# A new order of the work in one step of a fused recurrent block, with two squares and one product moved to VectorE

## The chip, the cores and the metric

The kernel runs on one core of a Trainium2 chip. The metric is the device time in microseconds (us) of one execution, as the median of a few runs. The profiled execution is one run of its own; its span and its engine rows come from the hardware profiler.

## What is computed

`x` holds 32 sequences of 256 tokens with 128 channels (8192 rows), all in float32. `xn` is the layer norm of `x`. Two branches start from it. The first is a time mix with the recurrent WKV sum over the tokens, followed by a channel mix; the second is a mixture of experts with one shared expert and, per token, one of eight routed experts (the top one, with input scaled by the sigmoid of its logit).

```
h  = ln(x);  xk, xv, xr = mixes of h and h one token before
k, v, r = xk @ Wk, xv @ Wv, sigmoid(xr @ Wr)
rwkv = r * wkv(k, v)                 # running max, exponentials, two scans, one division
x  = x + rwkv @ Wo
h  = ln(x);  xk, xr = mixes of h and h one token before
kk = square(relu(xk @ Fk))           # 128 -> 512 channels
x  = x + sigmoid(xr @ Fr) * (kk @ Fv)
out = x_in + x * silu(shared_expert(xn) + routed_expert(xn))
```

## The kernel before

The 8192 tokens are cut into 16 chunks of 512 (two sequences), and a prologue makes `xn`, its transpose `XT` and the router's logits for all of them. Then a loop of 18 steps runs; step i works on several chunks at once. The order of each engine's queue is written out by hand in one function `step(i)` per engine (`pe`, `act`, `dve`, `pool` below are TensorE, ScalarE, VectorE and GpSimd), and semaphores carry the waits. `fill(i, k)`, with k from 0 to 7, inserts the expert work that `plan()` assigned to that place: parts of the shared expert (S, D) in steps 0 to 5, one "slot" of the routed experts (E) at each of the eight places in steps 6 to 14, and the final products (Z) in steps 15 to 17. A slot is eight plus one plus four small matrix products on TensorE, three activations on ScalarE (`xh`, `px`, `xs`), one product on VectorE (`hx`) and one indirect DMA by GpSimd. Slot n on TensorE waits for `hx` of slot n-2; ScalarE's part of slot n waits for TensorE's part of slot n. Expert weights `ew` have five buffers.

In step i of the kernel before:

- `attention_out(i-1)` multiplies the `rw` of chunk i-1 by Wo; VectorE's `make_x2` adds xn, and takes the statistics (`x_bs`, `x_mv`); GpSimd's `rstd_of_x2` turns these into scale and shift (`x_sm`) in four small operations; ScalarE's `make_z2` applies them; then come `z2_transpose`, `make_h2` and VectorE's `channel_mixes`.
- the channel mix of chunk i-1 (`ffn_key` 0 to 3, `ffn_relu` 0 to 3, four squares into `kk`, 32 products `ffn_value`, `make_s`) is done whole at the end of the step, with the squares 0 and 2 on ScalarE and 1 and 3 on VectorE.
- `wkv_b` and `wkv_a` (two scans of 514 columns), `den_and_num` (two operations of 1024 columns) and `make_tn` belong to chunk i; `inverse_of_den` is a Ln and an Exp on ScalarE, and `make_rw` a product on GpSimd.
- for chunk i+1 the step makes `h1` (ScalarE), `d1` (GpSimd), `time_mixes` (three VectorE operations that read `D1` and `H1`), `key_value`, `running_max`, `differences` and `decays` (two Exp).

Ln and Exp live in another activation table than Silu and Tanh. ScalarE therefore loads a table at line 735 and loads the other one back at line 749, in each step. What stands between the two is called the stretch below; no expert work stands in it.

## Time and profile before

| | |
|---|---|
| runs (us) | 577.66, 577.74, 578.63; median 577.74 |
| profiled execution | 577.9, span 576.1 |
| TensorE busy | 464.0 us (81%) |
| VectorE busy | 425.2 us (74%) |
| ScalarE busy | 345.6 us (60%) |
| GpSimd busy | 264.7 us (46%) |
| mean DMA rate | 113 GB/s |

Read it as a pipeline in which no engine is full. The share of an engine says how much time a shorter wait could return at most; how long a step is follows from the waits between the engines.

### The profile page before, as it was taken

The page shows a single profiled execution, that of the slowest core. Times are in us where ns is not written, and L with a number is a line of the kernel's source. Part 1 is how long each engine was busy: PE and PEld are TensorE (multiplying, and loading weights), DVE is VectorE, ACT ScalarE, POOL GpSimd, SP SyncE. Part 2 cuts the span into 40 slices and gives each one's busy share as a digit, 9 for nine tenths or more (in the row PEclk, how much of TensorE's full clock was granted, in tenths as well). Part 3 has the DMA queues.
Part 4 walks back from the last instruction along what each step waited for, and adds up shares of the span by engine and source line. Part 5 has one row for each costly group of instructions (what it writes and reads, how often), then busy time and mean ns, then how long its engine had stood idle before and what let it go on. Part 6 is the DMA issues. An engine that isn't in the chain of part 4 may idle for free. (4 is left out here: it accounts for less than half of the span.)

```text
span 576.1 us, 8950 instructions
## 1 busy us (share of the span) xinstructions
PE 464.0 (81%) x2623; PEld 345.9 (60%) x2623; DVE 425.2 (74%) x836; ACT 345.6 (60%) x707; POOL 264.7 (46%) x317
## 2 busy tenths in 40 slices
PE   0989777797979797889898989898989897637661
PEld 0989244564646464787777777777777776425341
DVE  3553795879697977695969596969696968783766
ACT  3776423665646566676776677677777676536441
POOL 6664003657575858461818181818181828210100
PEclk9999988999899999999999999999999999957986
DMA  6329404010000001262727282727272825245482
GB/s 200 110 75 257 96 0 155 22 36 26 33 25 33 31 27 38 62 186 73 221 71 211 84 222 73 209 85 220 73 225 71 226 66 167 73 136 158 128 236 73
DMA packets 68864, 64.97 MB, mean 113 GB/s; under 512 B 5952, under 2 KB 57025, under 8 KB 68816
## 3 DMA queue, kind: packets, MB, share of 16 engines
q1 hardware_dynamic: 63344, 54.31, 34.5%
q0 software_dynamic: 4320, 8.53, 4.2%
q10 hardware_dynamic: 1152, 1.56, 0.8%
q8 instruction: 21, 0.34, 0.2%
q14 instruction: 27, 0.22, 0.1%
HBM read 46.86 MB, written 17.97 MB: 113 GB/s over the span
## 5 line engine op out<-in xcount | busy, mean ns | idle before, releaser
L849 POOL DMA_INDIRECT routed_out<-xh,xs x71 | 91.3, 1286 | 30.2 <-ACT xh L689 16.1
L486 PE MATMUL bank_ring<-xh,ew 128*128 128x128 f32 x568 | 78.6, 281 | 19.9 <-DMA ew<-ex_w 9.3
L486 PEld LDWEIGHTS bank_ring<-xh,ew 128*128 128x128 f32 x568 | 68.8, 191 | 26.9 <-ACT xh L689 15.2
L841 POOL DMA_INDIRECT tokens_by_expert<-xn,pos x64 | 67.2, 1051 | 37.0 <-issue 18.5
L1069 DVE TENSOR_TENSOR kk<-rk 128x512 f32<-128x512 f32 x32 | 26.3, 822 | 54.3 <-ACT rk L650 54.3
L689 ACT ACTIVATE xh<-bank_ring 128x256 f32<-128x256 f32 (+1 forms) x75 | 27.8, 371 | 63.4 <-PE bank_ring L500 62.3
L440 PEld LDWEIGHTS bank_out<-fvw,kk 128*128 128x128 f32 x512 | 60.9, 195 | 8.2 <-issue 8.2
L440 PE MATMUL bank_out<-fvw,kk 128*128 128x128 f32 x512 | 60.8, 278 | 0.0
L823 POOL TENSOR_SCALAR x_sm<-x_mv 128x4 f32<-128x4 f32 x16 | 3.8, 235 | 111.8 <-DVE x_mv L1051 111.8
L470 PE MATMUL bank_ring<-xt,sup 128*128 128x512 f32 x64 | 34.9, 628 | 17.5 <-DVE hs L1085 10.6
L837 POOL TENSOR_TENSOR rw<-den_num,lq 128x512 f32<-128x512 f32 x16 | 20.3, 1269 | 53.8 <-issue 46.5
L500 PE MATMUL bank_ring<-ew,hx 128*128 128x128 f32 x284 | 43.5, 276 | 0.7 <-DVE hx L1093 0.7
L449 PEld LDWEIGHTS bank_ring<-sdn,hs 128*128 128x128 f32 x256 | 31.6, 196 | 15.8 <-DVE hs L1085 12.0
L500 PEld LDWEIGHTS bank_ring<-ew,hx 128*128 128x128 f32 x284 | 38.1, 194 | 1.0 <-ACT xh L689 0.9
L1093 DVE TENSOR_TENSOR hx<-px,bank_ring 128x256 f32<-128x256 f32 x71 | 29.0, 408 | 13.1 <-ACT px L692 12.9
L431 PE MATMUL bank_fa<-xk,fkw 128*128 128x512 f32 x64 | 36.4, 653 | 2.3 <-ACT rk L650 2.3
L449 PE MATMUL bank_ring<-sdn,hs 128*128 128x128 f32 x256 | 32.3, 280 | 6.9 <-DVE hs L1085 6.9
L464 PE MATMUL bank_ring<-xt,sup 128*128 128x512 f32 x64 | 34.9, 628 | 2.3 <-ACT tg L668 2.3
L431 PE MATMUL bank_fb<-xk,fkw 128*128 128x512 f32 x64 | 34.3, 617 | 3.0 <-ACT tf L644 3.0
L1085 DVE TENSOR_TENSOR hs<-tg,bank_ring 128x512 f32<-128x512 f32 x32 | 21.7, 679 | 17.5 <-ACT tg L668 11.8
L470 PEld LDWEIGHTS bank_ring<-xt,sup 128*128 128x128 f32 x64 | 11.4, 193 | 38.7 <-DVE hs L1085 18.0
L572 ACT ACTIVATE xn<-xi,nb,rs 128x128 f32<-128x128 f32 x64 | 26.3, 482 | 12.1 <-POOL nb L801 11.9
(139 smaller groups left out, 1124.0 us busy)
## 6 DMA issues: line engine op xcount, KB each, us to landing
ew<-ex_w SPq DMA_DIRECT2D x71, 384.0 KB, 4.0
xi<-x SPq DMA_DIRECT2D x32, 256.0 KB, 3.7
tokens_by_expert<-pad_row SPq DMA_DIRECT2D x1, 4686.0 KB, 21.2
xs<-tokens_by_expert SPq DMA_DIRECT2D x71, 66.0 KB, 3.6
ew<-routed_out SPq DMA_DIRECT2D x16, 256.0 KB, 3.3
out<-xn SPq DMA_DIRECT2D x16, 256.0 KB, 3.2
routed_out<-xh,xs POOLq DMA_INDIRECT x71, 4.1
tokens_by_expert<-xn,pos POOLq DMA_INDIRECT x64, 2.3
```

What stands on the lines that cost most here:

```text
L431: nc.tensor.matmul((FA, FB)[q % 2][:, :], part(FKW, q, P), XK2[:, :], start=True, stop=True)\
L440: last = nc.tensor.matmul(part(BO, j, CH), KK[:, q * CHUNK + j * P:q * CHUNK + (j + 1) * P], part(FVW, q, CH), start=(q + j == 0), stop=(q ...
L449: last = nc.tensor.matmul(part(b, j, CH), h[:, q * CHUNK + j * P:q * CHUNK + (j + 1) * P], part(SDN, q, CH), start=(q == 0), stop=(q == EQ ...
L464: nc.tensor.matmul(ring(5 * m + 3 * q)[:, :], part(SUP, q, P), part(XT, m, CHUNK), start=True, stop=True)\
L470: nc.tensor.matmul(ring(5 * m + 3 * q + 1)[:, :], part(SUP, EQ + q, P), part(XT, m, CHUNK), start=True, stop=True).then_inc(s_su, 1)
L486: last = nc.tensor.matmul(part(GU[n % 2], q, P), part(w, q, P), xt[:, 0:P], start=True, stop=True)
L500: last = nc.tensor.matmul(BX[:, P:P + CH], part(h, q, P), part(w, 2 * EQ + q, CH), start=(q == 0), stop=(q == EQ - 1))
L572: last = nc.scalar.activation(xn_tile(t), part(XI[c % 4], j, P), ACT.Identity, bias=NB[:, t:t + 1], scale=RS[:, t:t + 1])
L689: nc.scalar.activation(XH[n % NXH][:, a:b], BX[:, a:b], ACT.Copy).then_inc(s_xh, 1)
L841: nc.gpsimd.indirect_dma_start(xs_dram, bass.IndirectOffsetOnAxis(ap=POS[:, t:t + 1], axis=0), XN[:, t * XROW:(t + 1) * XROW], None).then_ ...
L849: nc.gpsimd.indirect_dma_start(routed_dram, bass.IndirectOffsetOnAxis(ap=XS[(n - 2) % NXS][:, CH:CH + 1].bitcast(i32), axis=0), XH[n % NXH ...
L1093: nc.vector.tensor_tensor(HX[n % NHX][:, :], PX[n % 2][:, :], GU[n % 2][:, EF:2 * EF], ALU.mult)\
```

## The change

The same operations run, with three exceptions. Product `make_rw` moves from GpSimd to VectorE. VectorE makes the squares 2 and 3 and ScalarE the squares 0 and 1 (before: 1 and 3, 0 and 2). The router's sigmoid is now an Exp, a Ln and an Exp in the table that is loaded already, so one table load goes. The order within each step is new: the stretch with the table of Ln and Exp now stands at the start of step i and ends chunk i-1's attention there; the key products 2 and 3, their relus and squares, `ffn_value` and `make_s` of a chunk move into the following step; `time_mixes` stands directly behind `make_x2`; GpSimd makes `d1` ahead of `rstd_of_x2`. `X2` and `TR` get a second buffer, and the key products use the two banks in the order FA, FB, FB, FA. The three last Z items but one move from step 17 to step 16. What is cut from the diff are the semaphore values and the split of `differences`, `wkv_a`, `wkv_b` and `den_and_num` into shorter functions.

```diff
@@ -61,10 +61,9 @@
         steps[CHUNKS][k].append(item)
     for c in range(6):
         steps[CHUNKS - 1][c + 2].append(("Z", c))
-    for c in range(6, CHUNKS - 3):
-        steps[CHUNKS][c - 6].append(("Z", c))
-    for c in range(CHUNKS - 3, CHUNKS + 1):
-        steps[CHUNKS + 1][0].append(("Z", c))
+    for c in range(6, CHUNKS):
+        steps[CHUNKS][min(c - 6, 7)].append(("Z", c))
+    steps[CHUNKS + 1][7].append(("Z", CHUNKS))
     return steps
 
 
...
             def ffn_key(c, q):
                 if q == 0:
                     pe.wait_ge(s_mix2, 2 * c + 2)
-                    pe.wait_ge(s_tr, min(c + 2, CHUNKS))
+                    pe.wait_ge(s_tr, min(c + 3, CHUNKS))
                 elif q == 1:
                     pe.wait_ge(s_tf, c + 1)
+                elif q == 2:
+                    pe.wait_ge(s_rk, 4 * c + 2)
                 else:
-                    pe.wait_ge(s_rk, 4 * c + q - 1)
-                nc.tensor.matmul((FA, FB)[q % 2][:, :], part(FKW, q, P), XK2[:, :], start=True, stop=True)\
+                    pe.wait_ge(s_rk, 4 * c + 1)
+                nc.tensor.matmul(KB[q][:, :], part(FKW, q, P), XK2[:, :], start=True, stop=True)\
                   .then_inc(s_fk, 1)
 
-            def ffn_value(c):
-                if c > 0:
+            def ffn_value(c, a, b):
+                if a == 0 and c > 0:
                     pe.wait_ge(s_u, c)
-                for q in range(FQ):
-                    pe.wait_ge((s_kk, s_kd)[q % 2], 2 * c + 1 + q // 2)
+                for q in range(a, b):
+                    pe.wait_ge((s_kk, s_kd)[q // 2], 2 * c + 1 + q % 2)
                     for j in range(TPC):
                         last = nc.tensor.matmul(part(BO, j, CH), KK[:, q * CHUNK + j * P:q * CHUNK + (j + 1) * P],
                                                 part(FVW, q, CH), start=(q + j == 0), stop=(q + j == FQ + TPC - 2))
-                last.then_inc(s_kv, 1)
+                if b == FQ:
+                    last.then_inc(s_kv, 1)
 
...
@@ -512,36 +518,37 @@
 
             def step(i):
                 C, P1 = 0 < i <= CHUNKS, i + 1 < CHUNKS
+                if P1:
+                    z1_transpose(i + 1)
+                if i > 1:
+                    ffn_key(i - 2, 2)
+                    ffn_key(i - 2, 3)
+                    ffn_value(i - 2, 0, 2)
                 if C:
                     attention_out(i - 1)
+                if i > 1:
+                    ffn_value(i - 2, 2, FQ)
+                fill(i, 0)
                 if P1:
-                    z1_transpose(i + 1)
-                fill(i, 0)
+                    key_value(i + 1)
+                if C:
+                    z2_transpose(i - 1)
                 fill(i, 1)
+                if P1:
+                    receptance(i + 1)
                 fill(i, 2)
                 if i == 0:
                     routing_prefix()
                 fill(i, 3)
-                fill(i, 4)
-                if C:
-                    z2_transpose(i - 1)
-                fill(i, 5)
-                fill(i, 6)
                 if C:
                     ffn_receptance(i - 1)
+                    ffn_key(i - 1, 0)
+                fill(i, 4)
+                fill(i, 5)
+                if C:
+                    ffn_key(i - 1, 1)
+                fill(i, 6)
                 fill(i, 7)
-                if C:
-                    ffn_key(i - 1, 0)
-                    ffn_key(i - 1, 1)
-                if P1:
-                    key_value(i + 1)
-                if C:
-                    ffn_key(i - 1, 2)
-                    ffn_key(i - 1, 3)
-                if P1:
-                    receptance(i + 1)
-                if C:
-                    ffn_value(i - 1)
 
...
             def scores():
                 act.wait_ge(s_rt, RT_CHOSEN - 3)
                 act.wait_ge(s_tok, 1)
-                nc.scalar.activation(rows_of_xn[:, :, CH + 1], MX[:, :], ACT.Sigmoid).then_inc(s_sc, 1)
+                nc.scalar.activation(SC[:, :], MX[:, :], ACT.Exp, scale=-1.0).then_inc(s_sc, 1)
+                act.wait_ge(s_sc, 1)
+                nc.scalar.activation(SC[:, :], SC[:, :], ACT.Ln, bias=CST[:, K_ONE:K_ONE + 1]).then_inc(s_sc, 1)
+                act.wait_ge(s_sc, 2)
+                nc.scalar.activation(rows_of_xn[:, :, CH + 1], SC[:, :], ACT.Exp, scale=-1.0).then_inc(s_sc, 1)
 
...
@@ -711,42 +724,47 @@
 
             def step(i):
                 C, T, P1 = 0 < i <= CHUNKS, i < CHUNKS, i + 1 < CHUNKS
-                fill(i, 0)
+                if C:
+                    nc.scalar.preload_act_table_set("natural_log_exp_and_others")
+                    inverse_of_den(i - 1)
+                if i > 1:
+                    ffn_relu(i - 2, 2)
                 if P1:
                     make_h1(i + 1)
+                if i > 1:
+                    ffn_relu(i - 2, 3)
                 if T:
-                    tanh_d(i)
-                fill(i, 1)
+                    decays(i)
+                if i == 0:
+                    scores()
+                if i <= CHUNKS:
+                    nc.scalar.preload_act_table_set("silu_and_others")
+                if i == 0:
+                    tanh_d(0)
+                    receptance(0)
                 if C:
                     make_z2(i - 1)
+                fill(i, 0)
+                if C:
+                    make_h2(i - 1)
+                fill(i, 1)
+                if P1:
+                    receptance(i + 1)
                 fill(i, 2)
                 fill(i, 3)
-                if T:
-                    receptance(i)
-                fill(i, 4)
-                if C:
-                    make_h2(i - 1)
-                fill(i, 5)
-                fill(i, 6)
                 if C:
                     ffn_tanh(i - 1)
+                    ffn_relu(i - 1, 0)
+                    ffn_square(i - 1, 0)
+                fill(i, 4)
+                fill(i, 5)
+                if C:
+                    ffn_relu(i - 1, 1)
+                    ffn_square(i - 1, 1)
+                fill(i, 6)
                 fill(i, 7)
-                if T:
-                    nc.scalar.preload_act_table_set("natural_log_exp_and_others")
-                if C:
-                    ffn_relu(i - 1, 0)
-                    ffn_relu(i - 1, 1)
-                    ffn_square(i - 1, 0)
-                if T:
-                    inverse_of_den(i)
-                if C:
-                    ffn_relu(i - 1, 2)
-                    ffn_relu(i - 1, 3)
-                    ffn_square(i - 1, 2)
                 if P1:
-                    decays(i + 1)
-                if T:
-                    nc.scalar.preload_act_table_set("silu_and_others")
+                    tanh_d(i + 1)
 
...
-            def make_rw(c):
-                pool.wait_ge(s_tn, c + 1)
-                pool.wait_ge(s_iq, c + 1)
-                if c > 0:
-                    pool.wait_ge(s_att, c)
-                nc.gpsimd.tensor_tensor(RW[:, :], NUM, LQ[:, :], ALU.mult).then_inc(s_rw, 1)
...
@@ -864,24 +872,21 @@
 
             def step(i):
                 C, T, P1 = 0 < i <= CHUNKS, i < CHUNKS, i + 1 < CHUNKS
+                if P1:
+                    make_d1(i + 1)
                 if C:
                     rstd_of_x2(i - 1)
-                if P1:
-                    make_d1(i + 1)
-                for k in range(4):
-                    fill(i, k)
+                fill(i, 0)
                 if 0 < i < E_STEP:
                     scatter(12)
-                for k in range(4, 8):
+                for k in range(1, 8):
                     fill(i, k)
                 if i == 0:
                     pool.wait_ge(s_fill, 16)
                     pool.wait_ge(s_rt, RT_PLACED)
-                    pool.wait_ge(s_sc, 1)
+                    pool.wait_ge(s_sc, 3)
                     pool.wait_ge(s_tok, 1)
                     scatter(4)
-                if T:
-                    make_rw(i)
 
...
+            def make_rw(c):
+                dve.wait_ge(s_tn, c + 1)
+                dve.wait_ge(s_iq, c + 1)
+                if c > 0:
+                    dve.wait_ge(s_att, c)
+                nc.vector.tensor_tensor(RW[:, :], NUM, LQ[:, :], ALU.mult).then_inc(s_rw, 1)
...
@@ -1120,46 +1144,57 @@
 
             def step(i):
                 C, T, P1 = 0 < i <= CHUNKS, i < CHUNKS, i + 1 < CHUNKS
+                if T and i > 0:
+                    value_of_now(i)
+                if i + 2 < CHUNKS and i > 0:
+                    make_z1(i + 2)
+                if i > 1:
+                    ffn_square(i - 2, 2)
+                if C:
+                    make_rw(i - 1)
+                if i > 1:
+                    ffn_square(i - 2, 3)
                 if C:
                     make_x2(i - 1)
+                if P1:
+                    time_mixes(i + 1)
+                if T:
+                    exp_value(i)
                 fill(i, 0)
                 if i == 0:
                     routing_counts()
+                    value_of_now(0)
                 if T:
                     wkv_b(i)
-                fill(i, 1)
+                if i > 1:
+                    make_s(i - 2)
                 if T:
                     wkv_a(i)
-                fill(i, 2)
+                fill(i, 1)
                 if i == 0:
                     routing_starts()
+                if C:
+                    channel_mixes(i - 1)
+                fill(i, 2)
+                if T:
+                    weighted_sums(i)
+                fill(i, 3)
+                if i == 0:
+                    routing_rows()
                 if T:
                     den_and_num(i)
-                fill(i, 3)
-                if P1:
-                    time_mixes(i + 1)
-                if i == 0:
-                    routing_rows()
+                    make_tn(i)
                 fill(i, 4)
-                if C:
-                    channel_mixes(i - 1)
-                fill(i, 5)
-                if T:
-                    make_tn(i)
-                fill(i, 6)
-                if i + 2 < CHUNKS:
-                    make_z1(i + 2)
-                fill(i, 7)
-                if C:
-                    ffn_square(i - 1, 1)
                 if P1:
                     running_max(i + 1)
-                if C:
-                    ffn_square(i - 1, 3)
+                fill(i, 5)
                 if P1:
+                    difference_of_key(i + 1)
                     differences(i + 1)
-                if C:
-                    make_s(i - 1)
+                if i == 0:
+                    make_z1(2)
+                fill(i, 6)
+                fill(i, 7)
 
```

VectorE at the border of two steps with expert slots (`kk<-rk` is a square, `x<-bank_fb,xn` is `make_x2`, `d<-tf` and `xn<-d,x` are `make_s`, `hx` is a slot's product). Before:

```order
L1069 TENSOR_TENSOR kk<-rk 128x512
L999 TENSOR_TENSOR e<-bank_k,pp 128x2x256
L1000 SCALAR_TENSOR_TENSOR e<-pp,vectors 128x2x256
L1004 SCALAR_TENSOR_TENSOR dd<-pp,vectors,bank_k 128x512
L1074 SCALAR_TENSOR_TENSOR d<-tf,bank_out 128x512
L1077 SCALAR_TENSOR_TENSOR xn<-d,x 128x4x128
L1044 TENSOR_TENSOR x<-bank_fb,xn 128x512
L1047 BN_STATS x_bs<-x 128x6 x4
L1051 BN_AGGR x_mv<-x_bs 128x2 x4
L1093 TENSOR_TENSOR hx<-px,bank_ring 128x256
L1010 TENSOR_TENSOR ev<-e,bank_v 128x2x256
```

The step ends with `make_s`, and `rw` isn't VectorE's. The same border in the changed kernel:

```order
L982 TENSOR_TENSOR z<-xn,r 128x512
L1093 TENSOR_TENSOR kk<-rk 128x512
L1062 TENSOR_TENSOR rw<-den_num,lq 128x512
L1093 TENSOR_TENSOR kk<-rk 128x512
L1069 TENSOR_TENSOR x<-bank_fb,xn 128x512
L1072 BN_STATS x_bs<-x 128x6 x4
L1076 BN_AGGR x_mv<-x_bs 128x2 x4
L990 SCALAR_TENSOR_TENSOR xk<-d,vectors,h 128x512
L990 SCALAR_TENSOR_TENSOR xv<-d,vectors,h 128x512
L990 SCALAR_TENSOR_TENSOR xr<-d,vectors,h 128x512
L1019 TENSOR_TENSOR ev<-e,bank_v 128x2x256
L1117 TENSOR_TENSOR hx<-px,bank_ring 128x256
```

Both squares, `rw`, `make_x2` and the three mixes (`xk`, `xv`, `xr`) now stand in one row, and `make_s` has gone behind the first slot.

ScalarE in the stretch (`lq` is Ln, then Exp of the denominator, `rk` a relu, `h` is `make_h1`, `e` the decays, `z` is `make_z2`). Before:

```order
L735 ACT_TABLE_LOAD
L650 ACTIVATE rk<-bank_fa 128x512
L650 ACTIVATE rk<-bank_fb 128x512
L658 ACTIVATE kk<-rk 128x512
L620 ACTIVATE lq<-den_num,consts 128x512
L622 ACTIVATE lq<-lq 128x512
L650 ACTIVATE rk<-bank_fa 128x512
L650 ACTIVATE rk<-bank_fb 128x512
L658 ACTIVATE kk<-rk 128x512
L600 ACTIVATE e<-e 128x2x256
L602 ACTIVATE e<-e 128x2x256
L749 ACT_TABLE_LOAD
```

Four relus and two squares stand around the Ln and the Exp. The same stretch in the changed kernel:

```order
L728 ACT_TABLE_LOAD
L631 ACTIVATE lq<-den_num,consts 128x512
L633 ACTIVATE lq<-lq 128x512
L663 ACTIVATE rk<-bank_fb 128x512
L606 ACTIVATE h<-bank_k,vectors 128x2x256
L663 ACTIVATE rk<-bank_fa 128x512
L611 ACTIVATE e<-e 128x2x256
L613 ACTIVATE e<-e 128x2x256
L741 ACT_TABLE_LOAD
L640 ACTIVATE z<-x,x_sm 128x128 x4
L702 ACTIVATE xh<-bank_ring 128x256
```

Two relus and both squares left the stretch, `make_h1` came in, and `make_z2` stands ahead of the first slot behind it.

GpSimd in one step with shared-expert work (`rw` is `make_rw`, `x_sm` is `rstd_of_x2`, `d` is `make_d1`). Before:

```order
L823 TENSOR_SCALAR x_sm<-x_mv 128x4
L824 TENSOR_SCALAR x_sm<-x_mv 128x4
L826 TENSOR_TENSOR x_sm<-x_sm,minus_half 128x4
L829 TENSOR_TENSOR x_sm<-x_sm 128x4
L815 TENSOR_TENSOR d<-h 128x512
L841 DMA tokens_by_expert<-xn,pos 9088x132 x12
L837 TENSOR_TENSOR rw<-den_num,lq 128x512
```

The four small operations come first, and `rw` last. The same work in the changed kernel:

```order
L830 TENSOR_TENSOR d<-h 128x512
L838 TENSOR_SCALAR x_sm<-x_mv 128x4
L839 TENSOR_SCALAR x_sm<-x_mv 128x4
L841 TENSOR_TENSOR x_sm<-x_sm,minus_half 128x4
L844 TENSOR_TENSOR x_sm<-x_sm 128x4
L849 DMA tokens_by_expert<-xn,pos 9088x132 x12
```

`rw` is gone, and `d` moved ahead of the four small operations, which now run beside VectorE's three mixes.

## Rows read from the trace of the kernel before

**Rows 1.** Busy time by window: window, length, PE, PEld, DVE, ACT, POOL, PEclk, DMA, GB/s.

```profile
200.80:227.88 27.08, 23.81 (x119) 15.09 (x118) 22.68 (x37) 16.07 (x28) 17.79 (x19) 1.00 0.09 30
375.43:403.92 28.49, 25.53 (x175) 20.82 (x174) 22.48 (x41) 20.05 (x45) 14.11 (x14) 1.00 0.53 151
```

**Rows 2.** Timeline (start, length, engine, line), the table load of L735, steps 0 to 15.

```profile
95.89 1.28 ACT L735 ACT_TABLE_LOAD   x1
118.26 1.28 ACT L735 ACT_TABLE_LOAD   x1
...
227.88 1.28 ACT L735 ACT_TABLE_LOAD   x1
260.40 1.28 ACT L735 ACT_TABLE_LOAD   x1
...
487.97 1.28 ACT L735 ACT_TABLE_LOAD   x1
521.60 1.28 ACT L735 ACT_TABLE_LOAD   x1
```

**Rows 3.** Timeline, ScalarE, Ln and Exp of the denominator.

```profile
406.71 0.72 ACT L620 ACTIVATE lq<-den_num,consts 128x512 f32<-128x512 f32 x1
407.46 0.63 ACT L622 ACTIVATE lq<-lq 128x512 f32<-128x512 f32 x1
```

**Rows 4.** Timeline, a step with slots, from the output product to the second norm.

```profile
384.73 1.06 PE L408 MATMUL bank_fb<-att,rw 128*128 128x128 f32 x8
...
386.43 0.69 DVE L1044 TENSOR_TENSOR x<-bank_fb,xn 128x512 f32<-128x512 f32 x1
...
388.78 0.24 POOL L823 TENSOR_SCALAR x_sm<-x_mv 128x4 f32<-128x4 f32 x1 [7.78 <-DVE x_mv L1051]
...
389.29 1.04 POOL L826 TENSOR_TENSOR x_sm<-x_sm,minus_half 128x4 f32<-128x4 f32 x1
...
390.72 1.65 ACT L629 ACTIVATE z<-x,x_sm 128x128 f32<-128x128 f32 x4
```

**Rows 5.** Timeline, the same GpSimd operations in the steps 15 and 16.

```profile
502.80 1.97 POOL L826 TENSOR_TENSOR x_sm<-x_sm,minus_half 128x4 f32<-128x4 f32 x1
...
504.92 1.39 POOL L829 TENSOR_TENSOR x_sm<-x_sm 128x4 f32<-128x4 f32 x1
...
536.07 0.68 DVE L1100 TENSOR_TENSOR xn<-xt,xn 128x512 f32<-128x512 f32 x1
536.12 0.72 POOL L824 TENSOR_SCALAR x_sm<-x_mv 128x4 f32<-128x4 f32 x1
...
536.67 0.68 DVE L1105 TENSOR_TENSOR xt<-ew,xt 128x512 f32<-128x512 f32 x1
536.81 1.44 POOL L826 TENSOR_TENSOR x_sm<-x_sm,minus_half 128x4 f32<-128x4 f32 x1
```

**Rows 6.** Timeline, GpSimd operations of 512 columns beside VectorE's.

```profile
207.27 2.17 DVE L1000 SCALAR_TENSOR_TENSOR e<-pp,vectors 128x512 f32<-128x512 f32 x1
...
207.60 1.28 POOL L837 TENSOR_TENSOR rw<-den_num,lq 128x512 f32<-128x512 f32 x1
...
390.64 1.04 POOL L815 TENSOR_TENSOR d<-h 128x512 f32<-128x512 f32 x1
...
390.82 1.93 DVE L1016 TENSOR_TENSOR_SCAN bb_aa<-e,ev 128x514 f32<-128x514 f32 x1
```

**Rows 7.** Timeline, VectorE, the second scan of a step with shared-expert work.

```profile
189.07 1.20 DVE L1016 TENSOR_TENSOR_SCAN bb_aa<-e,ev 128x514 f32<-128x514 f32 x1
```

**Rows 8.** Timeline, TensorE, two slots in a row.

```profile
386.06 1.06 PE L486 MATMUL bank_ring<-xh,ew 128*128 128x128 f32 x8
...
387.51 1.06 PE L486 MATMUL bank_ring<-xh,ew 128*128 128x128 f32 x8
```

**Rows 9.** The page's DMA issues: the expert weights, KB each and us to landing.

```profile
ew<-ex_w SPq DMA_DIRECT2D x71, 384.0 KB, 4.0
```

**Rows 10.** Timeline, the end: the last 32 value products and the last VectorE operation.

```profile
560.77 3.73 PE L440 MATMUL bank_out<-fvw,kk 128*128 128x128 f32 x32
...
572.56 0.69 DVE L1110 TENSOR_TENSOR xn<-xn,xi 128x512 f32<-128x512 f32 x1
```

80 lines of the change are left out of this document (46 added, 34 removed).

## The prediction

> **What bounds the kernel now.** I read the busy time by window first. In a step with shared-expert work TensorE is busy 23.81 us of 27.08 and VectorE 22.68; in a step with expert slots it is 25.53 and 22.48 of 28.49 [rows 1]. No engine is full, so a step's length is set by a loop of waits, and a new order can win at most what lies above TensorE's work, some 3 us a step. The second view is the timeline of one row that occurs once in a step, the table load of line 735. Its starts give the periods: 22.4 us for step 1, 27.4 for each of steps 2 to 5, 32.5 for step 6 (where the slots begin, about 4 us more than a plain one), 28.45 for each of steps 7 to 14, 33.6 for step 15, and 54.5 us from the last load to the end of the span [rows 2]. The third view is the timeline inside the stretch and around `make_x2`, from which I take durations and the gaps between an end and the start it releases (about 0.05 us). I lay the new order out from these. Time 0 is the start of the first table load of the new step, which follows `tanh_d`.
>
> **The stretch in the new order.** ScalarE loads the table (1.28 us), then Ln and Exp follow, 0.75 us from start to start and 0.63 for the second [rows 2, 3], so the inverse is there at 2.7. Relus of the squares 2 and 3 end at about 3.2 and 4.3 with `h1` between them (it and each relu hold ScalarE some 0.6 us), and the second load ends near 6.7. VectorE has made the value product and `z1` by 1.3 and then waits for the relu until 3.2, because square 2 stands ahead of `rw`. `rw` costs about 0.68 there instead of 1.28 on GpSimd [rows 6] and ends at 4.5. The output product takes 1.06 [rows 4], so `make_x2` starts at 5.65. From its start to that of `z2` the old step took 390.72 - 386.43 = 4.3 us, and `z2` itself 1.65 [rows 4]. `z2` then runs from 10.0 to 11.6, if GpSimd is not held up. ScalarE's own queue puts the first slot or Silu behind it, and VectorE's queue puts that one's product ahead of the first scan. VectorE therefore goes on at 12.3, after 1.9, 0.6 and about 1.6 us of waiting: 4.1 us in a step, as much as the old order left (27.08 - 22.68 = 4.4).
>
> **Steps 2 to 5.** The old work of VectorE is 22.68 [rows 1]. Out goes the price of `rw` on GpSimd: the operation at line 1000 took 2.17 beside it [rows 6] where about 0.74 is its length at 0.60 a start and a like operation's 0.68 [rows 5], so 1.4. In comes `rw`, 0.6. The sum is 21.9, plus 4.1 of waits and some 0.6 of small gaps and the last wait for `tanh_d`: 26.6 us, against 27.4.
>
> **Steps 6 to 14.** From the first slot's product at 12.3 VectorE does that (0.3), the scan at 1.2, `make_s` (two operations, 1.4) and the second scan, which ends at 16.4. The second scan took 1.93 beside `d1` [rows 6] and takes 1.20 alone [rows 7]; `d1` now runs elsewhere, so that is a gain of 0.7. The second slot's product ends at 16.8 and releases TensorE's fourth slot. From there TensorE is full: five slots at 1.45 [rows 8], the 1.06 of the channel mix's receptance, for which I take the like product of [rows 4], and two key products of 0.85, 10.0 us in all, to 26.9. Five weight buffers, with 4.0 us from issue to landing [rows 9], hold the eighth slot until 4.3 us behind the end of the fifth, 0.5 more. ScalarE's part of the last slot and `tanh_d` add 1.5: 28.9 us, against 28.45.
>
> **What the mixes do to GpSimd.** This is the term that decides. The four small operations of `rstd_of_x2` took 1.9 us beside an operation that reads PSUM [rows 4]. Beside VectorE operations that read two SBUF tensors they took longer: in step 16 the second took 0.72 and the third 1.44, where the like forms took 0.24 and 1.04, so 0.9 more; in step 15 the third took 1.97 and the fourth 1.39 [rows 5], the fourth being short otherwise (the chain of four ends at 390.7 [rows 4], so under 0.35). In the old order VectorE did `hs` or `hx` and `ev` there, which read a bank. Now the three mixes stand directly behind the statistics, each reads `D1` and `H1`, and together they run 2.0 us. I take the 0.9 of step 16, since there too three such operations stood in a row. The bounds are 0 (as in the old steps) and 1.75 (the chain waits for all three mixes). VectorE waits for its first slot in any case, so the whole delay reaches the loop: 27.5 us for steps 2 to 5 and 29.8 for steps 6 to 14.
>
> [Rows 5] show GpSimd waiting for VectorE and [rows 6] VectorE for GpSimd. The Trainium skill (SBUF — State Buffer, "SBUF: two separate sides") says that the two share one pair of ports under a lock, that "DVE op in a 2-port perf mode, or with two SBUF inputs" and GpSimd operations exclude each other, and that the one that starts first keeps it. By that rule `d1`, released at 3.9 while `rw` runs since 3.8, would cost VectorE nothing; the row at 207.27 speaks against it, since that operation began 0.33 us ahead of GpSimd's and still ended 0.56 us behind it [rows 6].
>
> **The sum**, against the profiled time of 577.9 (the median of the runs is 577.74, 0.2 below). Step 0: about even; one table load of 1.28 goes, two tiny activations come, and the first mixes and `tanh_r` now stand ahead of the first Silu. Step 1: it has no squares or `make_s` to do (a full 27.5 less 2.6), so 24.9 against 22.4: +2.5, since part of step 0's work was taken over. Steps 2 to 5: 4 x 0.1 = +0.4. Steps 6 to 14: 9 x 1.3 = +11.7, with the 4 us of the start of the slots in both. Step 15: no mixes and no maximum; its channel mix is ready at about 15.2, then come six Z items (1.95 each, the first a third of it: 10.7) and `den_and_num` and `make_tn` (3.1), with 0.5 of small waits: 29.5 against 33.6, where the old one also paid for its GpSimd chain [rows 5]: -4.1. The end: 12.3 to the first product, four of these at 0.65, ten Z at 1.95 (19.5), `make_s` and `channel_mixes` of 1.4 and 2.1 make 37.9; relus, two squares and half of the value products (3.73 / 2 [rows 10]) add 3.7, the last sums 2.6, the store 576.1 - 573.25 = 2.85 [rows 10], and 3 for a TensorE that is slower when it has little to do: 50.0 against 54.5, -4.5. In all 577.9 + 2.5 + 0.4 + 11.7 - 4.1 - 4.5 = 583.9.
>
> **The rivals.**
>
> Free GpSimd (faster). If the four small operations slip in between the mixes at no cost, 14 steps lose the 0.9: 583.9 - 12.6 = 571.3. For it speaks that the old steps with the scans beside them show 1.04 for the third one [rows 4]. Against it stand all of [rows 5]. Chance 0.26.
>
> A half delay, 0.4 a step, as when only one of the four is caught: 583.9 - 7 = 577. Chance 0.12.
>
> The full wait (slower). The three mixes follow each other without a gap, and the chain starts only behind them: 1.75 a step instead of 0.9, so 583.9 + 14 x 0.85 = 595.8. The fourth operation of step 15, at 1.39, waited through a whole operation of VectorE [rows 5]. From 0.9 up each 0.1 us costs 1.4 us in all. Chance 0.15. The Trainium skill (SBUF — State Buffer, "SBUF: two separate sides") says that the other side fully blocks, which is this case if VectorE never lets go between two mixes.
>
> `d1` takes the port from `rw` or from square 3. Then `rw` ends 1.1 us later, as line 1000 did [rows 6], and with it `make_x2`: 583.9 + 15 x 1.1 = 600. Against it: VectorE's three operations follow each other closely, and [rows 6] had an operation with a bank ahead of line 1000. Chance 0.09.
>
> My own forecast has 0.38.
>
> **How the numbers follow.** Slower by over 0.2% (which is about what a measurement of this kernel can tell from no change, here 1.2 us): 0.38 + 0.15 + 0.09 = 0.62, the half delay split over all three with most on same: faster 0.30, same 0.08. The range reaches from just under the first rival to the full wait with 2 us on it: 569 to 598. Around the forecast alone, with the delay between 0.5 and 1.3, it would be 578 to 590.
>
> **What would show it.** Right: `x_sm` operations of 0.6 to 1.5 us beside `xk`, `xv` and `xr` in each step; `z2` about 5.2 us behind the start of `make_x2`; VectorE idle for 2 us and more before the first `hx` or `hs`; table loads 27.5 and 29.8 us apart; and the last 32 products followed by only one Z. Wrong: `z2` 4.3 us behind `make_x2` and loads 28.5 apart or less (the first rival), `rw` or square 3 longer than 1 us (the last), or a period set elsewhere, as by TensorE waiting for weights for over 1 us in each step. The end is wrong if the span behind the last first-load is not near 50.

## The result: slower, by more than forecast

The changed kernel took 607.07 us (median of 4 runs, 601.15 to 611.05) against 578.18 (577.66 to 579.81). One of the four, 611.05, fell into a slower state of the chip; the other three have a median of 605.45, and from them the ratio is 1.046 (95% interval 1.0375 to 1.0546). Forecast were 583.9 and a range of 569 to 598. The direction was right; the size lay outside the range. The profiled run of the changed kernel took 605.45 us with a span of 603.6, where the sum of the prediction had 582.1.

The head of its page, engines and the granted clock in 40 slices:

```profile
span 603.6 us, 8964 instructions
...
PE 476.6 (79%) x2623; PEld 361.5 (60%) x2623; DVE 430.1 (71%) x852; ACT 348.4 (58%) x708; POOL 260.0 (43%) x301
...
PEclk9999888999989999979898989898989898965898
```

The same table load as in [rows 2] gives the steps. Here it stands in line 728 and starts the step instead of standing behind it (timeline of ScalarE; start, length):

```profile
104.63 1.28 ACT L728 ACT_TABLE_LOAD   x1
130.09 1.28 ACT L728 ACT_TABLE_LOAD   x1
...
243.25 1.28 ACT L728 ACT_TABLE_LOAD   x1
281.21 1.28 ACT L728 ACT_TABLE_LOAD   x1
...
524.71 1.28 ACT L728 ACT_TABLE_LOAD   x1
555.38 1.28 ACT L728 ACT_TABLE_LOAD   x1
```

Period by period, in us (differences of the starts of this load, of which [rows 2] and the rows above show six each):

| part | before | predicted | after | after minus predicted |
|---|---|---|---|---|
| up to the first load (step 0) | 95.9 | 95.9 | 104.6 | +8.7 |
| step 1 | 22.4 | 24.9 | 25.5 | +0.6 |
| steps 2 to 5 | 109.6 | 110.0 | 113.2 | +3.2 |
| step 6 | 32.5 | 33.8 | 38.0 | +4.2 |
| steps 7 to 14 | 227.6 | 238.4 | 243.5 | +5.1 |
| step 15 | 33.6 | 29.5 | 30.7 | +1.2 |
| the end | 54.5 | 50.0 | 48.2 | -1.8 |

Two places that occur once, steps 0 and 6, hold 13 of the 21.5 us that the sum missed. Steps 7 to 14 hold another 5. (The column "predicted" takes eight steps of 29.8, which is 0.4 more than the sum had counted.) The first row is the least certain: in four kernels below that leave step 0 as it is, the first load comes at 101.6 to 106.0 us.

**The walk through the stretch held.** One step with slots of the changed kernel, the rows that answer to [rows 3, 4] (timeline; time 0 is 404.41):

```profile
404.88 1.95 PE L445 MATMUL bank_out<-fvw,kk 128*128 128x128 f32 x16
...
407.61 0.69 DVE L1093 TENSOR_TENSOR kk<-rk 128x512 f32<-128x512 f32 x1 [1.90 <-ACT rk L663]
408.22 0.68 DVE L1062 TENSOR_TENSOR rw<-den_num,lq 128x512 f32<-128x512 f32 x1
408.33 1.47 POOL L830 TENSOR_TENSOR d<-h 128x512 f32<-128x512 f32 x1 [2.90 <-ACT h L606]
408.82 1.53 DVE L1093 TENSOR_TENSOR kk<-rk 128x512 f32<-128x512 f32 x1
408.96 1.16 PE L411 MATMUL bank_fb<-att,rw 128*128 128x128 f32 x8 [2.13 <-DVE rw L1062]
409.95 3.45 PE L445 MATMUL bank_out<-fvw,kk 128*128 128x128 f32 x16
410.27 0.68 DVE L1069 TENSOR_TENSOR x<-bank_fb,xn 128x512 f32<-128x512 f32 x1
...
412.61 0.51 POOL L838 TENSOR_SCALAR x_sm<-x_mv 128x4 f32<-128x4 f32 x1 [2.81 <-DVE x_mv L1076]
...
413.19 0.57 POOL L839 TENSOR_SCALAR x_sm<-x_mv 128x4 f32<-128x4 f32 x1
...
413.74 1.51 POOL L841 TENSOR_TENSOR x_sm<-x_sm,minus_half 128x4 f32<-128x4 f32 x1
...
415.63 1.65 ACT L640 ACTIVATE z<-x,x_sm 128x128 f32<-128x128 f32 x4 [4.56 <-POOL x_sm L844]
...
417.84 0.42 DVE L1117 TENSOR_TENSOR hx<-px,bank_ring 128x256 f32<-128x256 f32 x1 [2.90 <-ACT px L705]
```

`make_x2` starts at 5.86 (predicted 5.65), `z2` 5.36 behind it where [rows 4] had 4.3, and the first slot's product at 13.4 (predicted 12.3 + 0.9). `z2` is 1.1 late, and the three operations ahead of it are the ones of [rows 5]: 0.51, 0.57 and 1.51 where [rows 4] have 0.24, a like one and 1.04. What the walk did not have stands in the row at 409.95: the second half of the value products took 3.45 us, as many instructions as the first half, ahead of the wait for `rw`, did in 1.95. TensorE's clock had fallen. This is so in two of the steps 7 to 13; in the other five the second half took 1.95 as well, and the clock fell later in the step (shown below).

**Step 0.** Timeline of TensorE and VectorE:

```profile
74.33 2.05 PE L392 MATMUL bank_v<-xv,att 128*128 128x512 f32 x2 [5.97 <-DVE tanh_d_and_value L1030]
...
79.59 0.69 DVE L1109 TENSOR_TENSOR hs<-tg,bank_ring 128x512 f32<-128x512 f32 x1 [3.11 <-PE bank_ring L476]
...
84.23 0.17 DVE L953 COPY rt<-bank_fb 128x8 f32<-128x8 f32 x1 [3.95 <-PE bank_fb L372]
```

TensorE's queue now has `key_value(1)` ahead of its second item. The value product needs bank_v, which `value_of_now(0)` reads last. On VectorE that operation stands behind the routing's counts (so it did before, as the end of `wkv_a`: it ran at 73.87, now at 73.54); new is that TensorE waits for it so early in its queue. TensorE idles 5.97 us, the shared expert's next product is late, and the routing's prefix behind it on TensorE's queue comes to VectorE at 84.23, where the kernel before had it at 75.30.

**Step 6.** The first transposes of the slots (ScalarE has to scale `xs` for them) stand behind `make_z2` on ScalarE:

```profile
254.47 1.65 ACT L640 ACTIVATE z<-x,x_sm 128x128 f32<-128x128 f32 x4 [4.55 <-POOL x_sm L844]
...
257.03 0.45 PE L499 MATMUL bank_ring<-consts,xs 128*128 128x128 f32 x1 [4.50 <-ACT xs L688]
...
260.87 0.42 DVE L1117 TENSOR_TENSOR hx<-px,bank_ring 128x256 f32<-128x256 f32 x1 [7.09 <-ACT px L705]
```

TensorE waits 4.50 us and VectorE 7.09 for a start of the pipeline that had cost some 4 us more than a plain step, and now costs 7 to 8. Behind the idle 4.50 us TensorE's clock was low too: 0.57 in the 8 us from 256 on, and 0.91 over the whole step, which ran at 1.00 before.

### The profile page after: what moved, and what is told of

It is laid out like the page before. It is cut to its first block, busy times and chain, and to the rows that moved or that the text cites. A ratio compares the mean times of both kernels' runs of the same rounds, so it can differ in the third digit from the quotient of the medians.

```text
span 603.6 us, 8964 instructions
## 1 busy us (share of the span) xinstructions
PE 476.6 (79%) x2623; PEld 361.5 (60%) x2623; DVE 430.1 (71%) x852; ACT 348.4 (58%) x708; POOL 260.0 (43%) x301
## 4 chain that ended last, share of the span: by engine, by line
PE 36%; DVE 22%; ACT 18%; issue 12%; POOL 9%; DMA 2%; ACTq 0%; POOLq 0%; DVEq 0%; SPq 0%
PE bank_ring L492 10%; PE bank_ring L506 5%; POOL x_sm L841 4%; DVE kk L1093 4%; ACT z L640 3%; ACT L728 3%; PE bank_fb L423 2%; DMA xi<-x 2%; DVE x_bs L1072 2%; ACT rk L663 2%; PE bank_fa L436 2%; PE bank_ring L455 2%; PE bank_fb L436 2%; ACT lq L631 2%; PE bank_ring L476 2%
## 5 line engine op out<-in xcount | busy, mean ns | idle before, releaser
L849 POOL DMA_INDIRECT tokens_by_expert<-xn,pos x64 | 72.3, 1130 | 47.1 <-DVE kk L971 26.7
L492 PEld LDWEIGHTS bank_ring<-xh,ew 128*128 128x128 f32 x568 | 77.0, 206 | 20.3 <-issue 11.8
L445 PEld LDWEIGHTS bank_out<-fvw,kk 128*128 128x128 f32 x512 | 69.3, 214 | 12.2 <-issue 8.8
L445 PE MATMUL bank_out<-fvw,kk 128*128 128x128 f32 x512 | 70.3, 297 | 3.2 <-DVE kk L1093 3.2
L640 ACT ACTIVATE z<-x,x_sm 128x128 f32<-128x128 f32 x64 | 26.4, 482 | 74.9 <-POOL x_sm L844 74.9
L1117 DVE TENSOR_TENSOR hx<-px,bank_ring 128x256 f32<-128x256 f32 x71 | 29.5, 416 | 51.0 <-ACT px L705 50.8
L702 ACT ACTIVATE xh<-bank_ring 128x256 f32<-128x256 f32 (+1 forms) x75 | 27.8, 370 | 48.5 <-PE bank_ring L506 45.4
L1093 DVE TENSOR_TENSOR kk<-rk 128x512 f32<-128x512 f32 x32 | 32.9, 1032 | 31.5 <-ACT rk L663 31.5
L830 POOL TENSOR_TENSOR d<-h 128x512 f32<-128x512 f32 x16 | 22.2, 1390 | 62.5 <-ACT h L606 62.5
L411 PE MATMUL bank_fb<-att,rw 128*128 128x128 f32 x128 | 19.9, 302 | 29.1 <-DVE rw L1062 29.1
L838 POOL TENSOR_SCALAR x_sm<-x_mv 128x4 f32<-128x4 f32 x16 | 7.6, 474 | 73.9 <-DVE x_mv L1076 73.9
L411 PEld LDWEIGHTS bank_fb<-att,rw 128*128 128x128 f32 x128 | 16.5, 201 | 32.2 <-DVE rw L1062 32.2
L455 PEld LDWEIGHTS bank_ring<-sdn,hs 128*128 128x128 f32 x256 | 30.9, 192 | 7.7 <-issue 6.2
```

The costliest lines, as they stand in the source:

```text
L411: last = nc.tensor.matmul(part(FB, j, CH), part(RW, j, P), part(ATT, 3, CH), start=True, stop=True)
L445: last = nc.tensor.matmul(part(BO, j, CH), KK[:, q * CHUNK + j * P:q * CHUNK + (j + 1) * P], part(FVW, q, CH), start=(q + j == 0), stop=(q ...
L455: last = nc.tensor.matmul(part(b, j, CH), h[:, q * CHUNK + j * P:q * CHUNK + (j + 1) * P], part(SDN, q, CH), start=(q == 0), stop=(q == EQ ...
L492: last = nc.tensor.matmul(part(GU[n % 2], q, P), part(w, q, P), xt[:, 0:P], start=True, stop=True)
L640: nc.scalar.activation(part(Z2, j, P), part(X2[c % 2], j, P), ACT.Identity, bias=SM2[:, 2 * TPC + j:2 * TPC + j + 1], scale=SM2[:, TPC + j ...
L849: nc.gpsimd.indirect_dma_start(xs_dram, bass.IndirectOffsetOnAxis(ap=POS[:, t:t + 1], axis=0), XN[:, t * XROW:(t + 1) * XROW], None).then_ ...
```

## The experiments

Twelve kernels, each timed beside the kernel before, whose median was 581.6 in the first four, 578.9 in the others. `time_mixes`, `make_rw` and the other names are those of the listing.

**Step 0 alone.** The value of step 0 goes back ahead of the first product on VectorE:

```diff
+                if i == 0:
+                    value_of_now(0)
                 fill(i, 0)
                 if i == 0:
                     routing_counts()
-                    value_of_now(0)
```

> The changed kernel with one edit in step 0: VectorE's value_of_now(0) stands ahead of the first Silu product and the routing counts, not behind them. Theory (the loss of step 0 is TensorE's value product of chunk 1, which now stands in TensorE's queue ahead of the second shared part and waits for value_of_now(0)): that product moves from 74.3 us to about 69.7, the routing prefix from 83.7 to about 78, and the table load of step 1 from 104.6 to 97 to 100; the time falls by 5 to 8 us. Rival (step 0 is longer because more VectorE work was put into it): the load of step 1 stays within 1.5 us of 104.6.

Measured: 599.98 us (ratio 1.033, 1.027 to 1.039), first load at 97.72 instead of 104.63; the steps behind it as in the changed kernel (7 to 13: 30.7 in the mean, for 30.8). One pair of executions gives 6.9 us for this one wait. Since the load comes at 101.6 to 106.0 without this edit, and at 99.4 and 99.6 in two later kernels that have it (100.8 and 101.8 in the last two, whose step 0 has more edits), the wait is worth some 4 to 7 of the 8.7 us of step 0; the rest is open.

**`rw` ahead of square 2** on VectorE:

> The changed kernel with VectorE's rw ahead of square 2 in each step, so that rw waits for the Exp alone (2.7 us behind the table load) and not for relu 2 (3.2). Theory (the loop runs from the table load over rw, the output product, make_x2, the second norm, the first slot and VectorE): each of 15 steps is about 1.1 us shorter, 10 to 16 us in all. Rival (steps are set by the work of VectorE or TensorE behind the first slot, so that the chain ahead of it is slack): under 3 us. A second outcome that the theory allows: GpSimd's d1 now meets the two squares, and takes the port from one of them; make_x2 would not notice, since it waits for the output product.

```diff
-                if i > 1:
-                    ffn_square(i - 2, 2)
                 if C:
                     make_rw(i - 1)
+                if i > 1:
+                    ffn_square(i - 2, 2)
```

Measured: 590.71 us (1.014, 1.007 to 1.022). In steps with slots TensorE waits 1.09 for `rw` instead of 2.13. But `make_x2` still stands behind square 3, and square 3 behind relu 3:

```profile
401.11 1.04 POOL L830 TENSOR_TENSOR d<-h 128x512 f32<-128x512 f32 x1 [2.89 <-ACT h L606]
...
401.54 1.16 DVE L1093 TENSOR_TENSOR kk<-rk 128x512 f32<-128x512 f32 x1 [0.29 <-ACT rk L663]
```

so it starts 5.43 into the stretch, only 0.43 sooner, and the shared steps gain just that: 27.46 against 27.90. Steps 7 to 13 gained 1.0: six of them ran at a clock of 1.00 and took 29.4 to 29.9 us, the one at 0.94 took 30.85. That was the first sign that the clock has a part in the difference.

**The first item of a step ahead of `make_z2`** on ScalarE (`fill(i, 0)` and `make_z2(i - 1)` change places):

> The changed kernel with ScalarE's fill 0 (the first slot's three activations, or the first Silu) ahead of make_z2 in each step. Theory (VectorE idles 2.9 us a step because the first hx or hs stands in its queue ahead of the first scan and its ScalarE part stands behind z2): hx comes about 2 us earlier in a step with slots, the idle time before it falls under 1.2 us, and steps 2 to 14 get about 1.5 to 2 us shorter; step 6 gains 4 us and more, since its first transposes stand behind the norm too; 20 to 30 us in all. Rival (z2 itself is what the rest waits for, by z2_transpose, h2 and the channel mixes): less than 5 us.

Measured: 594.02 us (1.024, 1.016 to 1.032). Step 6 takes 33.1 instead of 38.0 (and runs at a clock of 1.00, so a part of this is the clock), the shared steps 25.86 instead of 28.3, and the steps with slots gain nothing (30.9, steps 7 to 13, for 30.8): there TensorE waits for `rw`, for bank_v and for `z2` in turn, at a clock of 0.94 to 0.95.

**Is it the mixes that hold GpSimd's four small operations?** First `exp_value`, which reads a bank, went ahead of the mixes:

> The changed kernel with VectorE's exp_value (which reads PSUM) ahead of the three mixes (which read two SBUF tensors), nothing else. Theory (the mixes hold up the four small GpSimd operations of the second norm, 2.98 us instead of 1.90): the chain from the first to the end of the fourth takes 1.9 to 2.4 us, z2 starts 0.6 to 1.1 us earlier, and the time falls by 8 to 15 us. Rival (the long GpSimd chain costs nothing, since another wait ends last): the chain is shorter and the time stays within 3 us.

Measured: 599.96 us (ratio 1.035). Its timeline says that the edit didn't do what it was for:

```profile
408.87 0.23 POOL L838 TENSOR_SCALAR x_sm<-x_mv 128x4 f32<-128x4 f32 x1 [2.97 <-DVE x_mv L1076]
409.13 0.75 DVE L990 SCALAR_TENSOR_TENSOR xk<-d,vectors,h 128x512 f32<-128x512 f32 x1
409.19 0.78 POOL L839 TENSOR_SCALAR x_sm<-x_mv 128x4 f32<-128x4 f32 x1
...
409.94 1.51 POOL L841 TENSOR_TENSOR x_sm<-x_sm,minus_half 128x4 f32<-128x4 f32 x1
```

Only the operation that ran beside `exp_value` was short; the chain still took 2.9 us. So nothing on the port follows from this time. The next edit keeps the mixes off by a wait that the kernel doesn't need for its data:

```diff
+                if T:
+                    exp_value(i)
+                if C and P1:
+                    dve.wait_ge(s_nb2, i)
                 if P1:
                     time_mixes(i + 1)
-                if T:
-                    exp_value(i)
```

> The changed kernel with exp_value ahead of the mixes, as before, and with one wait added: VectorE makes the mixes only when GpSimd's four small operations have ended, so nothing holds them up. The wait costs VectorE time in which it had nothing to do but wait for the first hx. Theory (the shared port costs the loop 1.1 us a step): the four operations take 1.90 us instead of 2.98, z2 and the first hx come 1.1 us earlier, and steps 2 to 14 are 0.8 to 1.1 us shorter, 10 to 15 us in all, though a wait was added. Rival (the port's cost is hidden, and the added wait delays key_value on TensorE): the same or up to 10 us slower.

Measured: 588.64 us (1.0175, 1.0127 to 1.0224). Against the changed kernel that is 16 to 18 us less, but with two edits. The kernel of the run above has the same move of `exp_value` and not the wait, and took 599.96 (1.035, 1.027 to 1.044). **A wait was added and the kernel became 10 to 11 us faster.**

```profile
401.28 0.23 POOL L838 TENSOR_SCALAR x_sm<-x_mv 128x4 f32<-128x4 f32 x1 [2.81 <-DVE x_mv L1076]
401.59 0.23 POOL L839 TENSOR_SCALAR x_sm<-x_mv 128x4 f32<-128x4 f32 x1
...
401.79 1.04 POOL L841 TENSOR_TENSOR x_sm<-x_sm,minus_half 128x4 f32<-128x4 f32 x1
...
403.21 0.75 DVE L990 SCALAR_TENSOR_TENSOR xk<-d,vectors,h 128x512 f32<-128x512 f32 x1 [1.58 <-POOL x_sm L844]
```

The chain takes 1.90 us as in [rows 4]. At a full clock shared steps take 26.8 us, for 27.8 without the wait; steps 7 to 13 take 29.5 in the mean, for 30.0 without the wait and 30.8 in the changed kernel. VectorE pays 1.58 us of waiting, and the loop gains 1.0 in a shared step and 0.5 in one with slots.

**The three first edits together**, and then with the wait, and with `z2_transpose` and `make_h2` behind the second item:

> The changed kernel with three edits together: value_of_now(0) ahead in step 0, rw ahead of square 2, ScalarE's fill 0 ahead of make_z2. If the three gains are of different waits they add up: step 0 ends 6 us earlier, steps 2 to 5 come to 25.4 us (25.9 with the third edit alone, 0.4 from the second), step 6 loses 6 us, and the time is 30 to 36 us under the changed kernel's 605, so 570 to 576. If steps 7 to 14 are bound by TensorE instead (26 us of work, a wait for rw and one for z2), they stay near 29.5 us and the time comes to 576 to 582.

> All edits together, and z2_transpose on TensorE and make_h2 on ScalarE behind fill 1, so that TensorE does not stand idle for z2. If the waits named so far are all there is: step 0 at 98 us, steps 2 to 5 at 25 us, steps 7 to 14 at 27.5 to 28.5 us (26 us of TensorE work and the wait for rw), which gives 560 to 568 us, under both kernels. If TensorE's granted clock falls in the wait for rw and stays down for some of the products behind it, steps 7 to 14 stay over 29 us and the time is 572 or more.

Measured: 587.50 us (1.0135, 1.009 to 1.018) and 574.69 us (0.9926, 0.990 to 0.995). In the first the shared steps take 25.4 and step 6 32.2, but steps 7 to 13 still 31.2: by their ratios the three edits won some 7, 18 and 13 us alone and 19 together, each uncertain by some 5. The gains did not add; the one slot step of the seven that ran at a clock of 1.00 took 29.6, the other six 30.8 to 32.5. The second is the first to beat the kernel before, by 0.7%. In its slot steps the rows behind the first slot show a gap and a low clock (timeline of TensorE; the first row is the key product, the second the value product, the third the second slot):

```profile
391.64 1.36 PE L385 MATMUL bank_k<-xk,att 128*128 128x512 f32 x2 [2.33 <-DVE xk L990]
392.79 1.91 PE L392 MATMUL bank_v<-xv,att 128*128 128x512 f32 x2
394.50 1.69 PE L492 MATMUL bank_ring<-xh,ew 128*128 128x128 f32 x8
```

An idle 2.33 us, and behind it products of 1.91 and 1.69 that take 1.02 and 1.06 at full clock. Five of its steps 7 to 13 had such a stretch and took 30.1 to 31.2 us, the two at 1.00 took 29.3 and 29.5.

**The other side of moving `rw`**: the kernel before with only `make_rw` moved to VectorE, ahead of square 3.

> The kernel before with one part of the change alone: rw is made by VectorE, between running_max and square 3, where VectorE waits about 1 us. If VectorE's stretched operation at line 1000 (2.17 us beside GpSimd's rw in steps 2 to 5) was on the path that sets the end, five steps get 1.4 us shorter and the time falls by 5 to 8 us. Rival (make_s behind it waits for the 32 value products anyway, by 0.2 us in these steps and 1.5 us in those with slots): VectorE's operation is short again, its wait for bank_out grows by as much, and the time stays within 1.5 us.

Measured: 578.48 us against 578.86, ratio 0.9998 (0.9973 to 1.0024). The stretched operation of [rows 6], line 1000 at 2.17 us, goes (0.75 now) and the step gains nothing, since `make_s` behind it waits for the value products anyway (1.63 us instead of 0.20). In the old order the 1.4 us were hidden behind that wait. Whether they count in the new order, where `make_s` stands elsewhere, this run can't say.

**The clock by itself.** Extra products on TensorE while it waits for `rw`, written into the part of bank_fb that the output product then overwrites; ten, then four:

```diff
-                pe.wait_ge(s_rw, c + 1)
                 if c > 0:
                     pe.wait_ge(s_rk, 4 * c - 1)
+                    for j in range(10):
+                        nc.tensor.matmul(part(FB, j % TPC, CH), part(ATT, 3, CH), part(ATT, 3, CH),
+                                         start=True, stop=True)
...
+                pe.wait_ge(s_rw, c + 1)
```

> The changed kernel with ten extra 128x128 products on TensorE in each step from step 1 on, behind relu 2 of the channel mix and ahead of the wait for `rw`, into the part of bank_fb that the output product writes next (their values are overwritten, nothing is left out). They fill about 1.1 of the 2.1 us in which TensorE waits for `rw`. Theory 1 (the idle 2.1 us lowers the granted clock and that costs the slot steps about 0.6 us each): with TensorE at work there, the second half of the value products takes about 2 us instead of 3.45, the granted clock of a slot step goes from 0.94 towards 1.00, and the time falls by 5 to 9 us from 607.07, to about 600. Rival 1 (the clock is a result of something else, or the step is held by VectorE and ScalarE anyway): 607 within 1.5. Rival 2 (the extra products delay the output product): 608 to 612 us.

> The run e10_busy again with four extra products instead of ten: in e10 the ten took 2.4 to 2.5 us (a product of fp32 is two instructions, 0.12 us each) and held the output product 1.05 us behind `rw`, so `make_x2` came 0.8 us later in every step. Four take about 1.0 us, from relu 2 (2.6 us into the stretch) to 3.6, and `rw` ends at 4.5, so they hold nothing. Nothing is left out. In e10 the granted clock of the slot steps was 1.00 instead of 0.94 and they took 30.6 us instead of 30.4, although `make_x2` was 0.8 later, so theory 1 says that the clock alone is worth about 0.6 us in a slot step: shared steps as in the changed kernel (28.3), slot steps 29.8, in all 607.07 - 5 = about 602 us, the clock of a slot step at 0.98 to 1.00. Rival: the clock is worth nothing on the path: slot steps of 30.4 at any clock, 606 to 608 us. Second rival: four are too few, the clock stays at 0.94.

Measured: 614.57 us (ratio 1.062) and 605.12 us (1.044, 1.040 to 1.048). The ten took some 2.5 us instead of the 1.1 that I had counted and held the output product up, so the time went the wrong way; but every slot step ran at a clock of 1.00, and steps 7 to 13 took 30.8, with `make_x2` 0.8 us later. Three of the four shared steps fell to 0.94 and took 30.3 to 30.4. With four the answer is in the busy time by window, a step in a row (window, length, busy time of PE, PEld, DVE, ACT, POOL, granted clock, DMA, GB/s):

```profile
185.84:216.52 30.68, 27.39 (x127) 17.85 (x126) 22.79 (x38) 16.30 (x27) 17.70 (x17) 0.89 0.08 27
...
314.50:344.59 30.09, 26.20 (x183) 21.47 (x182) 22.95 (x41) 20.35 (x46) 14.54 (x14) 1.00 0.46 139
344.59:376.46 31.87, 27.83 (x183) 22.95 (x182) 23.09 (x41) 20.42 (x46) 14.39 (x14) 0.95 0.47 138
376.46:406.38 29.92, 26.19 (x183) 21.47 (x182) 22.96 (x41) 20.34 (x46) 14.31 (x13) 1.00 0.45 131
406.38:437.80 31.42, 27.57 (x183) 22.83 (x182) 23.03 (x41) 20.42 (x46) 14.78 (x14) 0.95 0.49 144
```

The same code, the same step, the same work on VectorE and ScalarE: 30.0 us at 1.00 and 31.4 to 31.9 at 0.95. With ten products it was 30.8, which fits the same 30.0 and the 0.8 of the late `make_x2`, though nothing shows that the two add. In the changed kernel itself the rows read so:

```profile
215.35:243.25 27.90, 23.63 (x120) 15.25 (x120) 22.75 (x38) 16.30 (x27) 17.80 (x18) 1.00 0.09 30
...
373.27:404.41 31.14, 26.52 (x175) 22.13 (x174) 23.12 (x41) 20.43 (x45) 14.17 (x13) 0.95 0.48 140
404.41:434.56 30.15, 26.42 (x175) 22.21 (x174) 22.96 (x41) 20.34 (x45) 14.79 (x14) 0.94 0.49 138
```

No slot step of it ran at 1.00; in the kernel before they did [rows 1]. But the step at 404.41 ran at 0.94 and took 30.15 us, hardly more than 30.0. What a low clock costs depends on where in the step it falls. Windows of 1 us put the low stretch of a slot step at one of two places. In the step from 404.41 it is the one seen above, behind the wait for `rw`. In the step from 373.27 the value products are short and the low stretch comes behind the waits for bank_v and `z2`:

```profile
378.81 1.95 PE L445 MATMUL bank_out<-fvw,kk 128*128 128x128 f32 x16
...
386.18 1.09 PE L417 MATMUL bank_fb<-consts,z 128*128 128x128 f32 x4 [1.15 <-ACT z L640]
387.06 1.91 PE L492 MATMUL bank_ring<-xh,ew 128*128 128x128 f32 x8
```

```profile
385.80:389.00 3.20, 2.82 (x14) 2.82 (x15) 2.27 (x4) 1.94 (x5) 1.74 (x1) 0.57 0.00 0
```

The second slot's product takes 1.91 us instead of 1.06, and the third slot starts 17.35 us into the step (390.62) where it starts at 15.72 in the other (420.13). Steps 7 to 13 of eight kernels, by where the low stretch starts (length of the step in us, number of steps):

| kernel | none, clock 1.00 | 4 to 7 us into the step | 10 to 15 us into the step |
|---|---|---|---|
| changed | | 30.1, 30.2 (2) | 30.7 to 31.3 (5) |
| step 0 alone | | 29.9 to 30.2 (4) | 31.3 to 31.9 (3) |
| `rw` ahead | 29.4 to 29.9 (6) | | 30.9 (1) |
| first item ahead | | 29.9 to 30.4 (4) | 31.5 to 32.5 (3) |
| `exp_value` ahead | 29.7 to 30.2 (4) | 30.0 to 30.4 (3) | |
| `exp_value` and wait | 28.9 to 29.8 (3) | 29.5 to 29.6 (4) | |
| three edits | 29.6 (1) | | 30.8 to 32.5 (6) |
| four extra products | 29.9 to 30.1 (5) | | 31.4, 31.9 (2) |

The early stretch costs under 0.5 us, the late one 0.7 to 2 us and more. The gap ahead of `rw` has a part in it, since none of the seven steps had a low stretch when ten products stood in it, and two had one with four. But it isn't the gap alone: where it was cut to 1.09 us, one late stretch came in the kernel with `rw` ahead and six with the three edits. What puts the fall at the one place or the other stays open.

The expected gain in total did not come (605.1 for 602): five of the seven slot steps 7 to 13 ran at 1.00 with four extra products, but two shared steps fell to 0.89 and took 30.7 us each. Why these fell, with TensorE busier than before, stays open. So the runs with extra products show the cost of the clock in a step, and not a gain of the kernel.

**Filling the gap instead.** On the kernel with all edits (574.69), TensorE's second item goes ahead of `key_value`, and VectorE's first product ahead of the mixes:

```diff
                 fill(i, 0)
+                fill(i, 1)
                 if P1:
                     key_value(i + 1)
-                fill(i, 1)
```

```diff
+                if i > 0:
+                    fill(i, 0)
                 if C and P1:
                     dve.wait_ge(s_nb2, i)
                 if P1:
                     time_mixes(i + 1)
```

> e7_combo (574.69 us) with TensorE's second item of a step placed ahead of the key and value products of the mixes, and with VectorE's first product of a step (`hx` or `hs`) ahead of its three mixes, in the time in which it waits for the statistics. Nothing is left out. In e7 TensorE idles 2.33 us in a slot step for `xk`, between the first slot and the key product, and the stretch behind it runs at a lower clock (value product 1.91 us instead of 1.02, second slot 1.69 instead of 1.06). Theory 1 (that gap is what the slot steps pay): a slot's 1.45 us fills it, the clock stays near 1.00 there, each of the 9 slot steps goes from 30.1 to about 28.7 us: 574.7 - 9 x 1.4 = about 562 us, and the shared steps stay at 26.2. Rival: slot steps are held by another wait (the last slots behind the weight buffers or the wait for `rw` at the border), so the gap only moves: 572 to 576 us.

Measured: 558.81 us (0.965, 0.961 to 0.969), slot steps 27.8 to 28.0 at a clock of 1.00. Last, on top of it, relu 3 ahead of `make_h1` on ScalarE:

> e9_slot_ahead (558.81 us) with ScalarE's relu 3 ahead of `make_h1` in the table-load stretch. Nothing is left out. In e9 VectorE does `rw`, square 2, waits 0.29 us for relu 3, does square 3 in 1.15 us (beside `make_d1` on GpSimd, which starts 0.44 earlier and follows `make_h1`) and only then `make_x2`, 0.75 us behind the end of the output product. Theory (the port and the queue): with relu 3 first, square 3 starts right behind square 2 and takes 0.69, `make_d1` starts 0.6 us later beside `make_x2`, which reads a bank; `make_x2` comes at 4.75 instead of 5.43 us, 0.6 to 0.7 us less in each of 15 steps: 549 to 551 us. Rival: the step is no longer bound by `make_x2` but by TensorE's work (25.1 of 27.8 us), 557 to 559 us. Second rival: `make_h1` and the decays come later and hold the value product or the scans: 559 to 565 us.

Measured: **548.01 us (547.37 to 549.15), ratio 0.946 (0.943 to 0.949)**, the fastest here. Its stretch, and a window over 27.00 of the 27.18 us of that slot step, to be held against the rows above:

```profile
369.22 0.69 DVE L1062 TENSOR_TENSOR rw<-den_num,lq 128x512 f32<-128x512 f32 x1 [1.46 <-issue]
...
369.83 1.29 DVE L1093 TENSOR_TENSOR kk<-rk 128x512 f32<-128x512 f32 x2
...
370.86 1.15 POOL L830 TENSOR_TENSOR d<-h 128x512 f32<-128x512 f32 x1 [3.39 <-ACT h L606]
...
371.16 0.69 DVE L1069 TENSOR_TENSOR x<-bank_fb,xn 128x512 f32<-128x512 f32 x1
```

```profile
366.45:393.45 27.00, 24.66 (x175) 20.73 (x174) 22.23 (x41) 20.35 (x45) 11.74 (x14) 1.00 0.55 156
```

Both squares take 1.29 together instead of 0.69 + 1.53, `make_x2` starts at 4.71 instead of 5.86, and a slot step takes 27.1 us, the kernel before 28.7 (steps 7 to 13 of both). The new order can be faster than the old one, once the waits that it had made for itself are gone. The gap was filled by two edits at once, and how much each of them, or any later edit without the earlier ones, would give wasn't tried.

## Why the prediction missed, step by step

- **Step 0, "about even".** This term failed most: +8.7 us. I looked at what was added and removed there (a table load, two activations) and never laid the queues of the step beside each other. `key_value(1)` ahead of the second item on TensorE is in the diff, and it waits for a read of bank_v that VectorE makes behind the counts, in the old order as in the new: a wait of 5.97 us. The first experiment took 4 to 7 us back; the rest of the 8.7 is open.
- **Step 6, "the 4 us of the start of the slots in both".** +4.2. The start was taken over as a constant, although the same walk had put `make_z2` ahead of ScalarE's first item. With that item ahead the step fell by 4.8 us, its clock back at 1.00 included.
- **The stretch.** Right: 5.86 for 5.65, 13.4 for 13.2.
- **GpSimd's delay, 0.9.** Right in kind, 1.1 in size, the same in every step from 2 to 14. The run with the added wait, held against the same order without it, shows that it reaches the loop: whole in the shared steps (1.0 us), by half in those with slots (0.5), where the prediction had it whole in both. The rivals of a free GpSimd (571) and of a half delay (577), 0.38 of the chances together, fell; so did the full wait of 1.75.
- **`d1` takes the port from square 3.** Listed as a rival with 1.1 us a step. It did take it, and `rw` stayed free (0.68): square 3 took 1.53, 0.84 more, of which 0.2 at most reach `make_x2`, because TensorE's output product runs meanwhile. The rival held in its mechanism and not in its price. By the rule of the Trainium skill (SBUF — State Buffer, "SBUF: two separate sides") the one that starts first keeps the port: `rw` began 0.11 us ahead of `d1` and was spared, square 3 began 0.49 behind it and was not, so here the trace agrees. `d1` itself took 1.47 us, and 1.04 in [rows 6]. With `rw` ahead of both squares the output product is done sooner and square 3 does hold `make_x2`: the last experiment moved relu 3, both squares then took 1.29 together, and `make_x2` came 0.72 us sooner.
- **Steps 2 to 5.** 27.90 for 27.5 in three of the four, and one at a clock of 0.94 with 29.46.
- **Steps 7 to 14.** 29.8 was the forecast; at a full clock such a step takes 30.0 (the rows of the run with four extra products), so the walk was near there too. The step that failed is a term that was not in the sum: TensorE's clock, taken as 1.00 from [rows 1] and allowed to be lower at the end alone. The walk has TensorE idle for `rw` and says nothing of its waits for bank_v and `z2`; behind one or the other the clock fell in each of these steps. The windows of steps 7 to 13 show 0.94 to 0.95 and 30.1 to 31.3 us, 30.8 in the mean; against 30.0 that is 5.5 us over seven steps, and the five with the late stretch hold 5.3 of it (step 14, with fewer slots, took 28.0). The 30.0 comes from another kernel, and the agreement is partly luck: the prediction had counted the whole delay of GpSimd here, of which half reaches the loop.
- **Step 15 and the end.** 30.7 for 29.5 and 48.2 for 50.0, together right within 0.6 by two errors of opposite sign. In step 15 the six Z items add up to 10.4 (5 x 1.95 and 0.65), not 10.7; at the end the 3 us for a slower TensorE had no row behind them.
- **The range.** Its upper end of 598 came from one mechanism (the port) and its bounds. The parts that occur once had no bound of their own, and those held 13 us; nor had the clock. The rival in which `d1` takes the port came to 600 by its own sum, above that end. And the chance of a half delay, 0.12, went to faster and same alone, though the text says that it is split over all three.

## What to carry to other kernels

When a change reorders every queue, lay out the first step and the step in which a new kind of work begins as carefully as the steady one: they occur once, but a wait there costs as much as half a microsecond in each of 16 steps. Where TensorE's queue is in order, ask for each product which operation of another engine frees its bank, and where that stands now. And a gap of some two microseconds on TensorE can cost another one or two in the step when the clock falls behind it: look in windows of 1 us where the low stretch lies before saying what it costs, and try an item that is ready in the gap.

## What the runs showed of the hardware

- Four GpSimd operations on 4 columns each take 1.90 us beside a VectorE operation that reads a bank and a scan, and 2.98 beside `scalar_tensor_tensor` operations that read two tensors in SBUF; each of the first three is longer (0.23 to 0.51, 0.23 to 0.57, 1.04 to 1.51), not one alone.
- An operation of VectorE that begins 0.43 to 0.49 us behind one of GpSimd's takes 1.16 to 1.53 us instead of 0.69.
- The granted clock of TensorE fell from the higher to the lower of its two levels, 2.4 and 1.2 GHz, for a stretch in each of the steps 7 to 14 of the changed kernel, at one of two places: directly behind an idle 2.13 us (0.64 over 4.5 us, window row below) or, in steps where it had not fallen there, some 8 us further into the step, behind waits of 0.87 and 1.15 us (0.57 over 3.2 us, row above). The first hardly lengthened the step, the second by 0.7 to 1.3 us, each against 30.0.
- An idle 1.09 us ahead of `rw` went with a clock of 1.00 in all of steps 7 to 13 of the two fastest kernels, and with a late low stretch in six of the seven with the three edits and five with all edits. So the length of this one gap doesn't decide.

```profile
408.90:413.40 4.50, 4.44 (x25) 4.44 (x26) 4.32 (x13) 2.15 (x3) 1.61 (x3) 0.64 0.01 4
```
